# Row maxima of the attention scores by a fused add-and-maximum on VectorE instead of mask products on TensorE

## What is computed

```python
diff = C + qa[:, None] - ka[None, :]
base = (diff >= 0) & (diff <= WINDOW)
scores = jnp.einsum('bhncd,bhnkd->bhnck', qc, kc) * SCALE
scores = jnp.where(mask[None, None], scores, -jnp.inf)
attn = jax.nn.softmax(scores, axis=-1)
out = jnp.einsum('bhnck,bhnkd->bhncd', attn, vc)
```

## Time and profile before

| | |
|---|---|
| median of 3 runs | 594.79 us (586.65, 594.79, 595.48) |
| the profiled execution's own time | 588.89 us |
| its span, first to last instruction | 587.1 us |
| TensorE, products | 498.7 us busy, 85% of the span |
| VectorE | 398.8 us, 68% |
| ScalarE | 280.4 us, 48% |
| GpSimd | 296.1 us, 50% |

### The profile page before, as it was taken

How to read it: one execution, slowest core, us unless ns; L and a number is a source line. 1 busy time by engine, 2 the same in 40 slices (tenths; PEclk the granted TensorE clock), 3 DMA queues, 4 the chain that set the end, 5 groups by cost and what they waited for, 6 DMA issues and landing times. The chain is left out here.

```text
span 587.1 us, 12428 instructions
## 1 busy us (share of the span) xinstructions
PE 498.7 (85%) x3571; PEld 469.8 (80%) x3571; DVE 398.8 (68%) x1153; ACT 280.4 (48%) x734; POOL 296.1 (50%) x330
## 2 busy tenths in 40 slices
PE   0586989998999989899751078899999999999996
PEld 0286989898988989889651067899999999999996
DVE  2698745444686787877777199977677677684575
ACT  1343655453455444463334375455555555653331
POOL 5553550201035553655567499844444444455994
PEclk9887989998999999999955569999999999999999
DMA  7133798796763754732395563343444443456951
GB/s 233 45 113 120 227 292 236 221 244 176 194 175 124 194 154 127 213 102 84 86 318 169 203 199 100 106 133 120 131 135 119 131 132 120 134 153 211 415 227 71
DMA packets 63479, 98.21 MB, mean 167 GB/s; under 512 B 10051, under 2 KB 48706, under 8 KB 62070
## 3 DMA queue, kind: packets, MB, share of 16 engines
q1 hardware_dynamic: 50328, 58.21, 36.6%
q0 software_dynamic: 9136, 32.53, 14.7%
q10 hardware_dynamic: 3950, 6.68, 3.6%
HBM read 60.69 MB, written 40.04 MB: 172 GB/s over the span
## 5 line engine op out<-in xcount | busy, mean ns | idle before, releaser
L1637 POOL DMA_INDIRECT ys_scr<-h,ids_st x59 | 60.8, 1031 | 67.9 <-DVE h L1691 64.1
L140 POOL DMA_INDIRECT xs_scr<-h,slot_u x64 | 62.5, 977 | 55.6 <-PE TB L1240 26.7
L105 PE MATMUL GU<-gu_hi,xT 128*128 x316 | 84.2, 348 | 1.8 <-DVE xT L1671 1.8
L105 PE MATMUL YP<-dn_hi,aT 88*128 x316 | 67.2, 305 | 4.0 <-DVE aT L1676 3.8
L1561 ACT ACTIVATE aT<-HT 88x256 fp32r<-88x256 f32 (+1 forms) x95 | 37.8, 399 | 65.8 <-PE HT L1797 65.8
L1683 DVE TENSOR_TENSOR h_act<-GU,g_act 128x176 f32<-128x176 f32 (+1 forms) x95 | 35.2, 370 | 47.5 <-ACT g_act L1554 47.5
L1250 PE MATMUL O<-raw,prob 128*128 128x99 f32 x512 | 67.1, 278 | 0.0
L857 ACT ACTIVATE prob<-TB 128x512 f32<-128x512 f32 x64 | 38.2, 597 | 57.3 <-PE TB L1240 56.5
L1250 PEld LDWEIGHTS O<-raw,prob 128*128 128x128 f32 x512 | 62.4, 194 | 0.1
L105 PEld LDWEIGHTS YP<-dn_hi,aT 88*128 88x128 f32 x316 | 47.6, 188 | 10.8 <-issue 7.2
L105 PEld LDWEIGHTS GU<-gu_hi,xT 128*128 128x128 f32 x316 | 52.2, 192 | 2.2 <-issue 2.2
(11 more groups left out here) (231 smaller groups left out, 1268.4 us busy)
## 6 DMA issues: line engine op xcount, KB each, us to landing
x_st<-xs_scr SPq DMA_DIRECT2D x79, 144.0 KB
dn_hi<-k_scr SPq DMA_DIRECT2D x48, 192.0 KB, 4.2
planes<-ys_scr POOLq DMA_DIRECT2D x8, 1024.0 KB, 16.9
k_scr<-raw SPq DMA_DIRECT2D x8, 768.0 KB, 6.1
dn_hi<-q_scr SPq DMA_DIRECT2D x24, 256.0 KB, 4.4
q_scr<-raw SPq DMA_DIRECT2D x8, 512.0 KB, 3.5
raw<-in_egu SPq DMA_DIRECT2D x8, 352.0 KB
raw<-in_x SPq DMA_DIRECT2D x36, 64.0 KB, 3.9
```

Source lines behind the costliest of these rows:

```text
L105: mm = eng.matmul(out, a, b, start=(i + j == 0), stop=(i == len(pairs) - 1 and j == 2))
L140: eng.indirect_dma_start(T["xs_scr"], bass.IndirectOffsetOnAxis(ap=T["slot_u"][:, par, t % 2, k:k + 1], axis=0), T["h2"][:, row, :], None) ...
L1637: eng.indirect_dma_start(ys, bass.IndirectOffsetOnAxis(ap=ids_st[:, r:r + 1].bitcast(U32), axis=0), results(r % 8), None).then_inc(sent[q] ...
```

## The change

`row_max` no longer takes one reduction over the four heads of a quarter. It issues one `tensor_tensor_reduce` for each head: the head's 128 columns of scores plus a tile `madd` of mask values (0 or minus 2 to the 100, 128 by 128, in SBUF), written back over the scores in the bank, with the maximum of the sum left in a column of `row_m`. In the built program each of them is two instructions, the sum over 128 by 128 and one that writes 128 by 1 into `row_m`.

In return `scores` has no product of the masks: the heads' products start the bank by themselves. `mask_qry` and its cast are gone. The minus sign that the reduction gave is now given by ScalarE's copy in `max_out` (`scale=-1.0`). `madd` is a new constant input, loaded by one transfer more on SyncE's queue at the start; VectorE waits for it once, ahead of the first `row_max`.

```diff
@@ first stage, SyncE and VectorE
         eng.dma_start(T["half"][:, :], A["halves"]).then_inc(k_ld, 16)
+        eng.dma_start(T["madd"][:, :], A["madd"]).then_inc(ma_ld, 16)
...
             eng.tensor_copy(mask_key[:, :], mk_raw[:, 0, :]).then_inc(cst, 1)
-            eng.tensor_copy(mask_qry[:, :], mk_raw[0:MASKS, 1, :]).then_inc(cst, 1)
@@ max_out, ScalarE
-            eng.activation(mT[:, p2, :], Y[0:HEADS, 0:P], ACT.Copy).then_inc(mt_cp, 1)
+            eng.activation(mT[:, p2, :], Y[0:HEADS, 0:P], ACT.Copy, scale=-1.0).then_inc(mt_cp, 1)
@@ row_max, VectorE
-            eng.tensor_reduce(neg_m[:, p2, 4 * q:4 * q + 4], SB[q % 2][:, :].rearrange("p (h x) -> p h x", h=4),
-                              AX.X, ALU.max, negate=True).then_inc(s_red, 1)
+            for hh in range(4):
+                head = 4 * q + hh
+                bank = SB[q % 2][:, hh * P:(hh + 1) * P]
+                done = eng.tensor_tensor_reduce(bank, bank, T["madd"][:, :], 1.0, -LEAST, ALU.add, ALU.max, row_m[:, p2, head:head + 1])
+            done.then_inc(s_red, 1)
@@ VectorE, ahead of the tiles
+        eng.wait_ge(T["ma_ld"], 16)
         for n in range(2):
             for q in range(4):
                 row_max(n, n, q)
@@ scores, TensorE
             bank = SB[q % 2]
-            eng.matmul(bank[:, :].rearrange("p (h x) -> p h x", h=4), mask_qry[:, :],
-                       mask_key[0:MASKS, :].unsqueeze(1).broadcast_to([MASKS, 4, P]), start=True, stop=True)
             for hh in range(4):
                 mm = eng.matmul(bank[:, hh * P:(hh + 1) * P], queries(n, t, 4 * q + hh), keys(par, 4 * q + hh, j),
-                                start=False, stop=True, skip_group_check=True)
+                                start=True, stop=True)
             mm.then_inc(s_mm, 1)
@@ transpose_max, TensorE
-            eng.transpose(Y[0:HEADS, 0:P], neg_m[:, p2, :], ident[:, :]).then_inc(mt_mm, 1)
+            eng.transpose(Y[0:HEADS, 0:P], row_m[:, p2, :], ident[:, :]).then_inc(mt_mm, 1)
```

More of the change, by code:

```diff
@@ L26 @@
 BIG = 2.0 ** 100
+LEAST = 2.0 ** 127
 HALF = 2 * DH
@@ L211, in project_qkv @@
     ident, iota_e, mod, VW, K2, MM = [T[x] for x in ("ident", "iota_e", "mod", "VW", "K2", "MM")]
-    mask_key, mask_qry, tri, r_hl, esc, wo_hl = [T[x] for x in ("mask_key", "mask_qry", "tri", "r_hl", "esc", "wo_hl")]
+    mask_key, tri, r_hl, esc, wo_hl = [T[x] for x in ("mask_key", "tri", "r_hl", "esc", "wo_hl")]
     q_scr, k_scr = T["q_scr"], T["k_scr"]
@@ L263, in project_qkv @@
     c_ld, wm_ld, w_ld, k_ld, e_ld = sem("c_ld"), sems("wm_ld", 2), sem("w_ld"), sem("k_ld"), sem("e_ld")
+    ma_ld = sem("ma_ld")
     c_exp, c_dve, c_col_done = sem("c_exp"), sem("c_dve"), sem("c_col_done")
@@ L274, in project_qkv @@
     T.update(valid_set=valid_set, k_ld=k_ld, e_ld=e_ld, z_st=z_st, cst=cst, mod_cp=mod_cp, wo_lo=wo_lo, qk_lo=qk_lo, qk_st=qk_st,
-             q0_ld=q0_ld, k0_ld=k0_ld, k1_ld=k1_ld, v_mm=v_mm, v_ev=v_ev, q_ev=q_ev, k_ev=k_ev, h1_ready=h1_ready)
+             q0_ld=q0_ld, k0_ld=k0_ld, k1_ld=k1_ld, v_mm=v_mm, v_ev=v_ev, q_ev=q_ev, k_ev=k_ev, h1_ready=h1_ready, ma_ld=ma_ld)
     block = T["block"]
@@ L520, in constants_and_out_weights @@
             eng.tensor_copy(r_hl[:, :, 0, :], r_raw[:, :, :]).then_inc(cst, 1)
-            eng.wait_ge(cst, 8)
+            eng.wait_ge(cst, 7)
             eng.tensor_tensor(r_hl[:, :, 1, :], r_raw[:, :, :], f(r_hl[:, :, 0, :]), ALU.subtract).then_inc(cst, 1)
@@ L629, in attention_and_routing @@
     ln_nm = sb("ln2_nm", [P, 2])
-    neg_m = sb("neg_m", [P, 2, HEADS])
+    row_m = sb("row_m", [P, 2, HEADS])
     mT = sb("mT", [HEADS, 2, P], F32R)
@@ L1293, in _ @@
         eng.wait_ge(q_spread, 2)
-        eng.wait_ge(T["cst"], 9)
+        eng.wait_ge(T["cst"], 8)
         eng.wait_ge(T["k0_ld"], 2 * LD)
@@ L1926, in program @@
             for name, shape, dt in (("mod", [P, 4, D], F32), ("esc", [P, 2, NE], F32),
-                                    ("mask_key", [MASKS + 1, P], F32R), ("mask_qry", [MASKS, P], F32R),
+                                    ("mask_key", [MASKS + 1, P], F32R),
                                     ("tri", [P, 2, P], F32R), ("r_hl", [P, KD, 2, 2 * NE], F32R),
-                                    ("half", [P, 2], F32)):
+                                    ("half", [P, 2], F32), ("madd", [P, P], F32)):
                 T[name] = shared.enter_context(nc.sbuf_tensor(name, shape, dt))
@@ L1956, in constants @@
     masks[:MASKS, 1, :] = np.where(np.concatenate([hidden, hidden], 1), -BIG, 0.0)
+    chunk = np.arange(CH)
+    seen = np.concatenate([chunk[None, :] >= chunk[:, None], chunk[None, :] <= chunk[:, None]], 1)
+    madd = np.where(np.concatenate([seen, seen], 0), 0.0, -BIG).astype(np.float32)
     tris = np.zeros((P, 2, P), np.float32)
@@ L1974, in constants @@
     return {"pads": rows(PLACES, NE * P), "spare": rows(PLACES + NE * P, 4 * P), "ids": (TOPK * ids).astype(np.float32),
-            "steps": steps.astype(np.float32), "ident": np.eye(P, dtype=np.float32), "masks": masks, "tris": tris, "halves": halves,
+            "steps": steps.astype(np.float32), "ident": np.eye(P, dtype=np.float32), "masks": masks, "madd": madd, "tris": tris, "halves": halves,
             "iotas": np.ascontiguousarray(iotas, dtype=np.float32)}
```

## The result

The changed kernel takes 639.32 us in the median (four runs, 636.76 to 647.19), the kernel before beside it 593.91 (586.65 to 595.48). The ratio is 1.079, 95% interval 1.0685 to 1.0895: slower, as forecast, but by 45 us and not by 20. The profiled execution took 640.42 us. (Medians here are over all runs, ratios over the undisturbed ones alone, so the two can differ a little.)

A forecast was written before the change was run, and what follows sets the result against it. It took TensorE to bound even tiles and VectorE odd ones. 588.9 (profiled execution) + 16.3 (tiles and start) + 6.5 (clock) = 611.7 us; the median's 5.9 more would give 617.6; it said 615, range 597 to 640.

The forecast's parts named there:

- The maxima's price: VectorE's row maxima: 1.12 us a quarter with the new pairs, against 0.60 for one reduction.
- h: VectorE's time per head for the new pair of instructions: 0.28 us, with bounds 0.21 and 0.46.
- Rival 2: VectorE's pair does not overlap: h from 0.36 to 0.46, time 630 to 650 us; chance 0.20.
- by far more than 20: Sign expected in the changed profile: VectorE's busy time up by far more than 20 us.
- Odd tiles: Odd tiles 3 to 13, where VectorE is the chain to `o_lo`: +2.0 us each, 12.0 in all.
- Even tiles: Even tiles 4 to 14, with waits ahead of `scores` 2 and the router: +0.6 us each, 3.6 in all.
- Nothing outside the attention: First stage, stretch after the last tile and experts unchanged; time moving outside the attention tiles would make the forecast wrong.
- ahead of tile 0: Maxima of tiles 0 and 1, before tile 0: from 0 to 4.2 us more, taken as +2.
- TensorE's clock: Longer `o_lo` waits bring 1.2 of 2.4 GHz for a stretch in each of tiles 5 to 13: +6.5 us.
- tiles 0 to 2: Tiles with VectorE's short list: mask products saved less a wait in tiles 1 and 2, -1.3 us together.
- the whole possible gain: TensorE's 64 mask products at 0.29 us: 18.6 us saved at most, only where TensorE sets the pace.

The follow-up runs named there:

- e2: Changed kernel with an overwritten product of the mask product's size put back ahead of each quarter of scores; 639.2 us, ratio to the kernel before 1.023.
- e3: Changed kernel with unread products in the waits ahead of `scores` 2, the router and, in odd tiles from 5 on, `o_lo`; 634.4 us, ratio 1.017.
- e5: Kernel before, unchanged, run again on another chip as control; 612.3 us, ratio 0.984.
- e8: Changed kernel with eleven unread 512-column products in TensorE's waits ahead of tile 0; 643.1 us, ratio 1.038 to the kernel before.
- e6: Changed kernel, unchanged, run again on another chip; 653.5 us, ratio not given.
- e16: e12 without the product ahead of each quarter, so only idle places are filled; 634.1 us, ratio 1.014 to the kernel before.
- e7: Kernel before with three more 128-column products of a head in place of each mask product, row maxima unmasked; 628.0 us, ratio 1.006.
- e9: Kernel before with `weigh` 1 moved ahead of the wait for `o_lo` in odd tiles from 3 on; 632.7 us, ratio 1.034.
- e1: Kernel before without its mask products, its reductions as they were, row maxima unmasked; 638.6 us, ratio 1.027.
- e12: Changed kernel with unread products ahead of tile 0, ahead of every quarter and in odd tiles' `o_lo` waits from 5 on; 624.1 us, ratio 1.013 to the kernel before.
- e14: Changed kernel, unchanged, as mark on the chip of e15 and e16; 653.4 us, ratio 1.030 to the kernel before.
- e15: e12 with four 128-column products for the one of 512 ahead of each quarter; 630.6 us, ratio 1.001 to the kernel before.
- e10: Changed kernel with `weigh` 1 moved ahead of the wait for `o_lo` in odd tiles from 3 on; 662.5 us, ratio 1.079 to the kernel before.
- e11: Changed kernel, unchanged, as control on the chip of e9, e10 and e12; 650.8 us, ratio 1.064 to the kernel before.
- e13: Kernel before with e12's unread products ahead of tile 0 and in odd tiles' `o_lo` waits from 5 on; 622.1 us, ratio 0.995.

## Why the prediction was right in direction and too small

Held, by its own steps:
- *The maxima's price.* h was said to be 0.28 us, measured 0.25: 0.33 for a sum and 0.14 for the read, overlapped. Rival 2 (0.46, no overlap) fell. The Trainium skill, "VectorE: DVE Perf Modes", section "The DRAIN you can't avoid", says that an instruction does not start before the pipeline is empty, but also that one which is not held starts earlier, which the prediction left out. This trace agrees with the second: a step of 0.25 us against 0.33 + 0.14 = 0.47. The prediction's price of a column was slightly off as well: its own rows, 0.68 and 0.43 us for 512 and 256 columns, give 0.98 ns and not 1.03, and h would be 0.30 by them instead of 0.28. VectorE's busy time grew by 22.0 us, not "by far more than 20".
- *Odd tiles.* At 0.25 the step's own sum gives 16 x 0.25 - 2.49 = 1.5 us a tile instead of 2.0; e2 shows +1.2 (13.44 over 12.3). The wait for `o_lo` was to be over 3 us; it is up to 2.64.
- *Even tiles.* +0.6 forecast, +0.26 at full clock (12.10 against 11.84), with the two waits that the step named. This rests on one tile too: other even tiles at 1.00 take up to 15.0 us on those chips (e3), with ScalarE's late `exps` in them.
- *Nothing outside the attention.* Behind tile 15 the span moved by -0.4 us.

Altogether the prices come to an estimated 9 to 11 us where 16.3 were forecast: 5 x 1.2 to 1.45 = 6 to 7.3 in the odd tiles 5 to 13, 0.6 in tile 3 (12.27 us in e2, 11.64 in e5, both at 1.00), 6 x 0.26 = 1.6 in the even ones, nothing in tiles 1 and 2 (10.3 and 10.7 us at 1.00 in e8, 20.9 together before), and 1.0 ahead of tile 0, where 2 were forecast. The last is the time from VectorE's first `row_max` to TensorE's first product of `scores_t`, 8.99 us in the kernel before and 10.01 in the changed one, 10.02 in e6, e8 and e16. Tile 0 then takes 6.8 us at full clock with and without the change (before, e8), and 12.3 at the lower level, so most of the +6.2 ahead of tile 1 is the clock's.

**The step that failed is "TensorE's clock"**: +6.5 us stood for what was about 40 (51.5 of the span less these 9 to 11). It was mis-sized in three ways.
1. *Where.* It placed low stretches in odd tiles 5 to 13 alone. Odd tiles gained 15.5 us in all, near the 12 + 6.5 forecast for them, but by luck: some 7 to 8 of it are prices and as much the clock's. But even tiles gained 21.5 and not 3.6, of which 20 are the clock's; tiles 1 and 2 gained 7.8, all of it the clock's, where tiles 0 to 2 were to give 1.3 back.
2. *How long.* It took 4 us a stretch from the earlier trace rows. The stretches last up to 27 us here and 31 and 34 in e6, e7 and e9, with TensorE busy 95 to 100% of these long ones. One tile with one stretch was no sample.
3. *What sets it off.* It took the single wait of 1.90 us in the earlier trace rows as the mark, and waits of 1.15 as harmless. Now low stretches begin in even tiles in which TensorE had waited only 0.50 and 0.47 us before (at 230.8 and 323.0 us), and e7 shows one with no wait before it. e1 shows that taking the products away is enough to lower the clock: the mask products' 18.6 us were entered as "the whole possible gain", while the time they filled helped to keep the clock. Taken away alone, they cost 2.7%.

The Trainium skill, "TensorE: Matmul & The Clock Gate", section "HAM oscillation — how this bites in real kernels", describes a kernel in which a wait that comes back in every tile, for a transfer of 3 to 5 us, brings the engine to its lower level each time, and advises to restructure so that the engine stays busy. These traces agree that waits which come back in every tile go with the lower level (0.99 to 0.75 over the tiles), with shorter waits than those. Staying busy was not enough here: in e5 TensorE was busy for 24.00 of 24 us at 0.51.

**Shown and not shown.** Shown: most of the loss goes with the clock and not with the work (e1, e12); the first stretch goes when the idle places ahead of tile 0 are filled (e8); filled waits and products in each quarter each give back a part of the clock (e14, e16, e15). Open: what sets a stretch off, since one comes after 17 us without a wait (e7); why a stretch lasts 3 us in one place and 34 in another; what lowered the clock in e9 and e10; and why the chips differ by 4 to 6% on the kernel before. A part of the last may be ScalarE's waits whose releaser the trace doesn't show, up to 2.9 us in e5 and 2.5 in e11, four in each. All traces of the later chips but e14's have some, the first chip's two have none. No run took them away.

## What to carry to other kernels

Before work is taken off TensorE, or a wait is put ahead of it, add up what TensorE's lower clock would cost over all of its tiles, not over the one with the wait: here the clock's part was some four times the prices. A kernel at 0.99 granted clock says nothing of how near it stands to the fall; the same kernel on another chip, or with 0.29 us less per quarter, fell. And compare granted clocks before durations: TensorE's busy time rose by 33.5 us with 64 products fewer.

## What was not expected of the hardware

- TensorE stays at its lower level while it is busy without a gap: 24.00 of 24 us at 0.51 (e5), after 17 us of nearly unbroken work at 0.99 the next 31 at 0.51 (e7).
- Filling idle places with products that nobody reads made a kernel 27 us faster (e12 against e11), and in the kernel before it raised the clock from 0.87–0.90 to 0.90–0.92 with no loss of time (e13).
- A `tensor_tensor_reduce` with an accumulator output costs a step of 0.25 us for 128 columns, its read of 0.14 us hidden behind the next sum.
- The same program took 594, 616, 620, 625 and 627 us in the median on five chips.
